# A DLRM tower on one core: features mixed before the projection, row norms from a Gram matrix, products repacked by DMA

## The chip, the core and the metric

The kernel runs on one core of a Trainium2 chip. The core has five engines with an instruction list each: TensorE (PE, matmuls; its weight loads are listed as PEld), VectorE (DVE), ScalarE (ACT), GpSimd (POOL) and SyncE (SP, which here only starts DMAs). They wait for each other by semaphores. The metric is the device time of one execution in microseconds, the median of repeated runs. All arithmetic is float32.

## The reference

512 samples; each has 256 dense features and 26 sparse ids. Each id picks a row of 64 numbers out of a table. Cut to what matters:

```python
e = stack([tbl_f[ids[:, f]] for f in range(26)], axis=1)       # 512 x 26 x 64
x = layer_norm(dense @ Wd.T, gd, bd)                           # 512 x 128
y = layer_norm(einsum('bnd,ed->bne', e, Ws), gs, bs)           # 512 x 26 x 128, norm over e
y = einsum('bne,pn->bep', y, Wsi)                              # 512 x 128 x 32: 26 features mixed to 32
y = swapaxes(layer_norm(y, gsi, bsi), 1, 2)                    # norm over the 32
T = concatenate([x[:, None, :], y], axis=1)                    # 512 x 33 x 128
Z = einsum('bnd,bmd->bnm', T, T)                               # all products of pairs of rows
z = layer_norm(Z[:, TRIL_I, TRIL_J] @ Wl.T, gl, bl)[:, :384]   # 528 pairs -> 512, first 384 kept
h = concatenate([z, dense], axis=1)
h = maximum(h @ W_top1 + b_top1, 0)
h = maximum(h @ W_top2 + b_top2, 0)
out = h @ W_top3                                               # 512 x 1
```

A layer norm subtracts the mean and multiplies by 1/sqrt(variance + 1e-5), then scales (g) and shifts (b).

## The kernel before

The batch is cut into 32 units of 16 samples; 8 units make a block of 128 samples, 4 blocks in all. Every engine's list is written by hand as a loop of steps `step(t)`, in which the stages of different units stand beside each other (unit t in one stage, t-1 and t-2 in later ones). Most buffers are double, by the unit's parity.

A unit goes through these stages. POOL gathers table rows by indirect DMA into `g_sb` (128 rows of 64 numbers each time, two side by side in a slot; 104 gathers). PE turns a slot (`transposes`, L240), ScalarE copies it to `sT` (`rows_out`, L426). PE multiplies by the centred Ws (`project`, L247, two matmuls of 256 columns into `psA`). ScalarE squares and sums each 128 numbers (`squares_a`, L431) and takes the root (L439); VectorE inverts it (L584) and scales by it and by gs into `y1` (`norm_a`, L591). PE mixes the 26 features with the centred Wsi and adds bs by a further row (`mix`, L260, four matmuls of 128 columns into `psB`). ScalarE squares (L446), VectorE sums over 32 (L598), ScalarE takes the root (L452), VectorE inverts it (L603), multiplies into `T` (`norm_b`, L609), and then multiplies `T` by gsi (L615) and adds bsi (L621, or on POOL L221 for every fourth unit). ScalarE puts x into `T` as its first column (`enter_x`, L460). PE forms the products, 16 matmuls of 32x32 (`inner`, L270, into `psZ`), and ScalarE spreads them over the partitions of `Zt` in four copies (`keep_z`, L468):

```python
src = psZ[(m % 2) * PROJ:(m % 2 + 1) * PROJ, :].rearrange("p (s q j) -> p s q j", s=US, j=JQ)
for q in range(4):
    dst = Zt[q * PROJ:(q + 1) * PROJ, u // BU, :, m * US:(m + 1) * US].rearrange("p j s -> p s j")
    last = act.activation(dst, src[:, :, q, :], ACT.Copy)
```

Once a block is there, `linear` (L286) multiplies by Wl in 32 matmuls of 128 columns, cut into pieces that stand in the following steps; `linear_sums` (L294) adds squares, and the three top layers follow (`layer1` L323 and L326, `layer2` L337, `output` L344). The dense part of the first layer (`dense_part`, L305) is computed once. SyncE loads the weights, each behind an early gather; POOL waits for a slot of `g_sb` to be free, as there are 13 slots.

## Time and profile before

| | us |
|---|---|
| time, median of 3 runs | 308.99 (307.81 to 311.92) |
| span of the profiled execution | 212.3 |
| PE busy | 180.5 |
| PE weight loads busy (beside PE) | 155.4 |
| ScalarE busy | 151.7 |
| VectorE busy | 134.3 |
| POOL busy | 110.8 |

The span goes from the first to the last instruction of one profiled execution. That execution's own time is not on record; the timed runs are longer than the span by what lies before and after the program's instructions. Busy times of different engines overlap; the time is set by the chain of waits that ends last.

### The profile page before, as it was taken

To read this page: it belongs to the slowest core of one execution; us is meant where nothing else is said; L and a number is where in the kernel's file an instruction comes from. 1 tells how busy PE (TensorE), PEld (TensorE's weight loads), DVE (VectorE), ACT (ScalarE), POOL (GpSimd) and SP (SyncE) were. 2 spreads that over 40 slices of the span, in tenths; PEclk is the share of its full clock that TensorE was granted. 3 is DMA by queue.
4 is the path that set the end of the run, shared out by engine and by line. 5 is a ranking of instruction groups with operands and counts; after the bars stand their busy time and mean duration, and the time that the engine had idled before them with its cause. 6 is when DMAs were issued, how large, how long until landed. Compare 5 with 4: busy or idle time off the path is not lost.

```text
span 212.3 us, 5428 instructions
## 1 busy us (share of the span) xinstructions
PE 180.5 (85%) x1994; PEld 155.4 (73%) x1994; DVE 134.3 (63%) x360; ACT 151.7 (71%) x597; POOL 110.8 (52%) x116
## 2 busy tenths in 40 slices
PE   0557635879989969998989999899979999999996
PEld 0535433556666658887878998799969999989894
DVE  0234891276878796778877888766777788910401
ACT  2033843889999988999988999967779978590122
POOL 1777777714777677377787867777750200000000
PEclk9985995899999999999999999999999999999999
DMA  5345663310111011101111111111110000000000
GB/s 185 119 124 144 193 210 103 93 47 2 33 26 28 12 27 27 20 19 24 29 23 25 29 25 20 23 30 23 28 25 3 0 3 0 5 3 0 0 3 0
DMA packets 4942, 9.21 MB, mean 43 GB/s; under 512 B 1842, under 2 KB 2098, under 8 KB 4916
## 3 DMA queue, kind: packets, MB, share of 16 engines
q0 software_dynamic: 3328, 3.41, 8.2%
q1 hardware_dynamic: 1298, 4.69, 6.8%
q10 hardware_dynamic: 290, 0.76, 1.0%
q8 instruction: 16, 0.26, 0.6%
q14 instruction: 10, 0.08, 0.1%
HBM read 8.86 MB, written 0.00 MB: 42 GB/s over the span
## 4 chain that ended last, share of the span: by engine, by line
PE 56%; ACT 18%; issue 10%; POOL 9%; DMA 5%; DVE 1%; ACTq 0%
PE psW L286 13%; PE psZ L270 12%; POOL g_sb L214 9%; PE psA L247 8%; ACT Zt L468 7%; PE psB L260 7%; ACT square L431 3%; DMA g_sb<-in_table,row_id 3%; PE psT L240 3%; PE psW L294 2%; DMA ids_sb<-in_ids 2%; PE psA L326 2%; ACT sqB L446 2%; ACT sdB L452 1%; PE psB L326 1%
## 5 line engine op out<-in xcount | busy, mean ns | idle before, releaser
L214 POOL DMA_INDIRECT g_sb<-in_table,row_id x104 | 101.9, 980 | 30.8 <-issue 28.7
L468 ACT ACTIVATE Zt<-psZ 32x128 f32<-32x128 f32 x128 | 48.9, 382 | 4.2 <-PE psZ L270 2.7
L270 PEld LDWEIGHTS psZ<-T 128*32 128x32 f32 x1024 | 34.9, 112 | 10.9 <-issue 8.6
L270 PE MATMUL psZ<-T 128*32 128x32 f32 x1024 | 37.9, 196 | 4.4 <-issue 3.3
L247 PE MATMUL psA<-ws_c,sT 128*104 128x256 f32 x128 | 35.3, 399 | 4.8 <-ACT sT L426 4.4
L431 ACT ACTIVATE square<-psA 104x128 f32<-104x128 f32 x128 | 33.4, 280 | 6.9 <-PE psA L247 6.7
L260 PE MATMUL psB<-wsi_c,y 105*128 105x128 f32 x256 | 36.2, 285 | 0.8 <-DVE y L591 0.4
L591 DVE SCALAR_TENSOR_TENSOR y<-psA,rA,rows_sb 104x128 f32<-104x128 f32 x128 | 35.7, 340 | 0.1
L286 PEld LDWEIGHTS psW<-Zt,wl_sb 128*128 128x128 f32 x256 | 31.4, 192 | 5.9 <-ACT Zt L468 2.8
L286 PE MATMUL psW<-Zt,wl_sb 128*128 128x128 f32 x256 | 32.5, 276 | 3.5 <-ACT hd L554 1.6
L260 PEld LDWEIGHTS psB<-wsi_c,y 105*128 105x128 f32 x256 | 32.4, 197 | 2.9 <-DVE y L591 2.1
L603 DVE RECIPROCAL rB<-sdB 128x16 f32<-128x16 f32 x32 | 8.1, 252 | 39.3 <-ACT sdB L452 39.3
L247 PEld LDWEIGHTS psA<-ws_c,sT 128*104 128x104 f32 x128 | 20.9, 177 | 14.5 <-ACT sT L426 7.6
L426 ACT ACTIVATE sT<-psT 128x256 f32<-128x256 f32 (+1 forms) x32 | 10.8, 338 | 24.0 <-PE psT L240 23.9
L431 ACT ACTIVATION_READ_ACCUMULATOR square<-psA 104x1 f32 x128 | 27.3, 213 | 0.0
L609 DVE TENSOR_TENSOR T<-psB,rB 128x512 f32<-128x512 f32 x32 | 22.0, 687 | 0.5 <-PE psZ L270 0.4
L615 DVE TENSOR_TENSOR T<-T,rows_sb 128x512 f32<-128x512 f32 x32 | 21.8, 681 | 0.1
L598 DVE TENSOR_REDUCE ssB<-sqB 128x16 f32<-128x512 f32 x32 | 21.6, 676 | 0.0
L240 PE MATMUL psT<-small_sb,g_sb 128*128 128x128 f32 x52 | 13.6, 315 | 8.4 <-DMA g_sb<-in_table,row_id 8.4
L221 POOL TENSOR_TENSOR T<-T,rows_sb 128x512 f32<-128x512 f32 x7 | 8.2, 1173 | 23.6 <-DVE T L615 23.6
L446 ACT ACTIVATE sqB<-psB 128x512 f32<-128x512 f32 x32 | 18.8, 586 | 0.6 <-PE psB L260 0.2
L621 DVE TENSOR_TENSOR T<-T,rows_sb 128x512 f32<-128x512 f32 x25 | 17.0, 680 | 0.0
(82 smaller groups left out, 165.0 us busy)
## 6 DMA issues: line engine op xcount, KB each, us to landing
wl_sb<-in_wl SPq DMA_DIRECT2D x4, 512.0 KB, 3.9
g_sb<-in_table,row_id POOLq DMA_INDIRECT x104, 2.5
w_sb<-in_w SPq DMA_DIRECT2D x2, 512.0 KB, 3.5
w_sb<-in_w SPq DMA_DIRECT2D x1, 768.0 KB, 5.9
small_sb<-in_small SPq DMA_DIRECT2D x1, 635.5 KB, 6.2
dense_sb<-in_dense ACTq DMA_DIRECT2D x1, 512.0 KB, 3.8
rows_sb<-in_rows ACTq DMA_DIRECT2D x1, 224.0 KB, 5.4
ids_sb<-in_ids SPq DMA_DIRECT2D x1, 104.0 KB, 4.1
```

The lines of the kernel that those rows point to most:

```text
L214: pool.indirect_dma_start(g_sb[:, k % SLOTS, h * DSP:(h + 1) * DSP], None, table, bass.IndirectOffsetOnAxis(row_id[:, 2 * k + h:2 * k + h ...
L247: mm = pe.matmul(psA[m % 2][0:ROWS, g * 2 * E:(g + 1) * 2 * E], sT[:, (2 * m + g) * ROWS:(2 * m + g + 1) * ROWS], ws_c[:, :], start=True, ...
L260: mm = pe.matmul(psB[m % 2][:, g * P:(g + 1) * P], y1[:, m % 2, g, :], wsi_c[:, :], start=True, stop=True)
L270: mm = pe.matmul(psZ[(m % 2) * PROJ:(m % 2 + 1) * PROJ, s * PROJ:(s + 1) * PROJ], T[:, m % 2, s, 1:1 + PROJ], T[:, m % 2, s, 0:PROJ], star ...
L286: mm = pe.matmul(psW[b % 2][:, f * BS + s0:f * BS + s1], wl_sb[:, j, f * P:(f + 1) * P], Zt[:, b, j, s0:s1], start=(j == 0), stop=(j == JQ ...
L431: last = act.activation(square[0:ROWS, m % 2, g, :], psA[m % 2][0:ROWS, g * E:(g + 1) * E], ACT.Square, accum_out=ssA[0:ROWS, m % 2, g:g + 1])
L446: act.activation(sqB[:, m % 2, :], psB[m % 2][:, :], ACT.Square).then_inc(B_squared, 1)
L468: last = act.activation(dst, src[:, :, q, :], ACT.Copy)
L591: last = dve.scalar_tensor_tensor(out=y1[0:ROWS, m % 2, g, :], in0=psA[m % 2][0:ROWS, g * E:(g + 1) * E], scalar=rA[0:ROWS, m % 2, g:g + 1 ...
L598: dve.tensor_reduce(ssB[:, m % 2, :], sqB[:, m % 2, :].rearrange("p (s j) -> p s j", j=PROJ), AX, ALU.add).then_inc(B_summed, 1)
L609: dve.tensor_tensor(T[:, m % 2, :, 1:], psB[m % 2][:, :].rearrange("p (s j) -> p s j", j=PROJ), rB[:, m % 2, :].rearrange("p (s o) -> p s ...
L615: dve.tensor_tensor(T[:, m % 2, :, 1:], T[:, m % 2, :, 1:], gsi_b.rearrange("p (o j) -> p o j", o=1).broadcast_to([P, US, PROJ]), ALU.mult ...
```

## The change

The stages up to `T` are put in another order, and the unit is now 32 samples (two halves of 16, on partitions 0 to 63 and 64 to 127), 16 units in 4 blocks.

- Mixing comes first: `mix` takes the gathered rows as they lie (`g_sb` as weights, 128 rows) and a masked copy of Wsi for each of the 13 slots of a half block (`wsi_x`) into `psU`, four matmuls of 64 to 192 columns for a unit. Then `project` multiplies by Ws times gs (`ws_g`), and adds bs times the sums of Wsi by matmuls with one row.
- The first norm needs the length of each row after the projection. It is taken from the row itself: `norms` multiplies the turned rows by the 64x64 matrix Ws Ws^T (`gram`), VectorE multiplies by the row and sums over 64 (`mult_a`, `sums_a`), ScalarE takes the root, VectorE inverts it and scales the gathered rows in place (`scale_a`).
- gsi and bsi are no longer applied to `T`. Their products go into the weights of the last linear layer (`wl_g`, and extra rows from `shift_part` and `x_sum`), gl and bl into those of the first top layer (`w1_g`, `bias_part`).
- `inner` forms 32x33 products (a column of ones is in front), in four groups on four ranges of partitions; ScalarE copies each group (8 samples) to `Zs`, and seven DMAs per block (`relay`) put five columns at a time on the partitions of `Zt`. `linear` is then five matmuls of 512 columns with the samples on partitions, its norm is taken by bn_stats on VectorE, and three transposes (`turn`) bring it back.
- All 52 slots of gathered rows are kept; gathers wait for nothing. `psT`, `psG`, `psU`, `psZ`, `psW` and `psH` are single; `psB` is a pair that holds the two halves of one unit. POOL has only the gathers.

```diff
+BLOCKS, BU, HS, US = 4, 4, 64, 16
+UNITS = BLOCKS * BU
+BS = 2 * HS
+SLOTS = HS * NSP // P
+ALL_SLOTS = BLOCKS * SLOTS
+NEW = ((0, 4), (4, 7), (7, 10), (10, 13))
...
+            def relay(b):
+                sp.wait_ge(Z_kept, 4 * BU * (b + 1))
+                if b == 0:
+                    sp.wait_ge(fills, 4)
+                for q in range(7):
+                    sp.dma_start(Zt[BASE[q]:BASE[q] + ROWS[q], b, :, :],
+                                 Zs[FIRST[q] - 1:PROJ, b % 2, CW * q:CW * (q + 1), :]).then_inc(d_zt[b], 16)
...
-            def gathers(lo, hi):
-                for k in range(lo, hi):
-                    if k >= SLOTS:
-                        pool.wait_ge(pair_transposed, k - SLOTS + 1)
-                    for h in range(2):
-                        pool.indirect_dma_start(
-                            g_sb[:, k % SLOTS, h * DSP:(h + 1) * DSP], None, table,
-                            bass.IndirectOffsetOnAxis(row_id[:, 2 * k + h:2 * k + h + 1], 0),
...
+            for k in range(ALL_SLOTS):
+                for h in range(2):
+                    pool.indirect_dma_start(
+                        g_sb[:, k, h * DSP:(h + 1) * DSP], None, table,
+                        bass.IndirectOffsetOnAxis(row_id[:, 2 * k + h:2 * k + h + 1], 0),
+                    ).then_inc(gathered[k], 16)
...
-            def project(u, m):
...
+            def norms(u):
+                lo, hi = NEW[u % BU]
                 pe.wait_ge(sT_ready, u + 1)
-                if u >= 2:
-                    pe.wait_ge(y1_ready, u - 1)
-                for g in range(2):
-                    mm = pe.matmul(psA[m % 2][0:ROWS, g * 2 * E:(g + 1) * 2 * E],
-                                   sT[:, (2 * m + g) * ROWS:(2 * m + g + 1) * ROWS], ws_c[:, :],
+                if u == 0:
+                    pe.wait_ge(gram_ready, 2)
+                else:
+                    pe.wait_ge(A_mul, u)
+                for n in range(hi - lo):
+                    mm = pe.matmul(psG[:, n * P:(n + 1) * P], sT[:, u % 2, n * P:(n + 1) * P], gram[:, :],
                                    start=True, stop=True)
-                mm.then_inc(A_done, 1)
-
-            def mix(u, m):
-                pe.wait_ge(y1_ready, u + 1)
+                mm.then_inc(G_done, 1)
...
-                for g in range(UG):
-                    mm = pe.matmul(psB[m % 2][:, g * P:(g + 1) * P], y1[:, m % 2, g, :], wsi_c[:, :],
-                                   start=True, stop=True)
-                mm.then_inc(B_done, 1)
...
+                ps_ = pieces(j)
+                for n, (c, lo, hi) in enumerate(ps_):
+                    s0 = first_sample(c)
+                    mm = pe.matmul(psU[:, (lo - US * j) * PROJ:(hi - US * j) * PROJ], g_sb[:, SLOTS * b + c, :],
+                                   wsi_x[:, c, lo - s0:hi - s0, :], start=(n == 0), stop=(n == len(ps_) - 1),
+                                   skip_group_check=True)
+                mm.then_inc(U_done, 1)
...
+            def project(u):
+                pe.wait_ge(U_ready, u + 1)
+                if u == 0:
+                    pe.wait_ge(d_bs0, 16)
+                    pe.wait_ge(d_bs1, 16)
+                    pe.wait_ge(x_tr, 1)
+                else:
+                    pe.wait_ge(T_ready, 2 * u)
+                for h in range(2):
+                    pe.matmul(psB[h][:, :], bs_sb[32 * h:32 * h + 1, :], wsum[32 * h:32 * h + 1, :],
+                              start=True, stop=False)
+                for h in range(2):
+                    pe.matmul(psB[h][:, :], ws_g[h * DSP:(h + 1) * DSP, :], U[h * DSP:(h + 1) * DSP, u % 2, :],
+                              start=False, stop=True).then_inc(B_done, 1)
...
-                for s in range(US):
-                    mm = pe.matmul(psZ[(m % 2) * PROJ:(m % 2 + 1) * PROJ, s * PROJ:(s + 1) * PROJ],
-                                   T[:, m % 2, s, 1:1 + PROJ], T[:, m % 2, s, 0:PROJ], start=True, stop=True)
...
+                for gq in range(4):
+                    h = gq // 2
+                    if gq % 2 == 0:
+                        pe.wait_ge(T_ready, 2 * u + h + 1)
+                    if u:
+                        pe.wait_ge(Z_kept, 4 * (u - 1) + gq + 1)
+                    for n in range(GQ):
+                        s = (gq % 2) * GQ + n
+                        mm = pe.matmul(psZ[gq * PROJ:(gq + 1) * PROJ, n * COLS:(n + 1) * COLS],
+                                       T[:, u % 2, h, s, 2:2 + PROJ], T[:, u % 2, h, s, 0:COLS],
+                                       start=True, stop=True)
+                    mm.then_inc(Z_done, 1)
...
-                for n in range(lo, hi):
-                    f, j = n // JQ, n % JQ
-                    mm = pe.matmul(psW[b % 2][:, f * BS + s0:f * BS + s1], wl_sb[:, j, f * P:(f + 1) * P],
-                                   Zt[:, b, j, s0:s1], start=(j == 0), stop=(j == JQ - 1))
...
+                for jj in range(CW):
+                    mm = pe.matmul(psW[:, :], Zt[0:KL, b, jj, :], wl_g[0:KL, jj, :], start=(jj == 0),
+                                   stop=(jj == CW - 1))
...
+            def turn(b):
+                pe.wait_ge(z_normed, b + 1)
+                if b:
+                    pe.wait_ge(y_copied, b)
+                for k in range(KZ):
+                    mm = pe.transpose(psH[:, k * P:(k + 1) * P], zn[:, k * P:(k + 1) * P], eye_sb)
+                mm.then_inc(z_tr, 1)
...
+            def bias_part():
+                pe.wait_ge(d_w1, 16)
+                for f in range(K1):
+                    for k in range(KZ):
+                        mm = pe.matmul(psH[:, f:f + 1], w1_sb[:, k, f * P:(f + 1) * P], bl_c[:, k:k + 1],
+                                       start=(k == 0), stop=(k == KZ - 1))
+                mm.then_inc(bz_done, 1)
+
+            def shift_part():
+                pe.wait_ge(am_ready, 1)
+                pe.wait_ge(d_wl, 16)
+                for jj in range(CW):
+                    mm = pe.matmul(psW[0:NA, :], am[0:KL, jj, :], wl_sb[0:KL, jj, :], start=(jj == 0),
+                                   stop=(jj == CW - 1))
+                mm.then_inc(m_done, 1)
...
+                if t + 1 < UNITS:
+                    transposes(t + 1)
+                if t < UNITS:
+                    mix(t)
+                if t + 1 < UNITS:
+                    norms(t + 1)
+                if 1 <= t:
+                    inner(t - 1)
+                if t < UNITS:
+                    project(t)
+                if t == 0:
+                    x_sum()
+                if t == 1:
+                    shift_part()
                 if t == 2:
...
+                if t in (3, 4):
+                    dense_part(2 * (t - 3))
+                    dense_part(2 * (t - 3) + 1)
+                b, j = (t - 5) // BU, (t - 5) % BU
+                if 0 <= b < BLOCKS - 1:
+                    if j == 0:
+                        linear(b)
+                    if j == 1:
+                        turn(b)
+                        layer1(b, 0, K1 // 2)
+                    if j == 2:
+                        layer1(b, K1 // 2, K1)
+                        layer2(b)
+                    if j == 3:
+                        output(b)
+
+            for t in range(UNITS + 1):
...
+            def rows_out(u):
+                lo, hi = NEW[u % BU]
+                act.wait_ge(tr_done, u + 1)
...
+                act.activation(sT[:, u % 2, 0:(hi - lo) * P], psT[:, 0:(hi - lo) * P], ACT.Copy).then_inc(sT_ready, 1)
...
-            def squares_a(u, m):
-                act.wait_ge(A_done, u + 1)
-                for g in range(UG):
-                    last = act.activation(square[0:ROWS, m % 2, g, :], psA[m % 2][0:ROWS, g * E:(g + 1) * E], ACT.Square,
-                                          accum_out=ssA[0:ROWS, m % 2, g:g + 1])
-                last.then_inc(A_summed, 1)
...
+            def keep_u(u):
...
+                act.activation(U[:, u % 2, :], psU[:, :], ACT.Copy).then_inc(U_ready, 1)
...
-                src = psZ[(m % 2) * PROJ:(m % 2 + 1) * PROJ, :].rearrange("p (s q j) -> p s q j", s=US, j=JQ)
-                for q in range(4):
-                    dst = Zt[q * PROJ:(q + 1) * PROJ, u // BU, :, m * US:(m + 1) * US].rearrange("p j s -> p s j")
-                    last = act.activation(dst, src[:, :, q, :], ACT.Copy)
...
+                lo = 2 * US * j + GQ * gq
+                act.activation(Zs[:, b % 2, 0:COLS, lo:lo + GQ].rearrange("p c s -> p s c"),
+                               psZ[gq * PROJ:(gq + 1) * PROJ, 0:GQ * COLS].rearrange("p (s c) -> p s c", s=GQ),
+                               ACT.Copy).then_inc(Z_kept, 1)
...
+                if t + 1 < UNITS:
+                    rows_out(t + 1)
+                if t < UNITS:
+                    enter_x(t)
+                    keep_u(t)
+                if 1 <= t:
+                    keep_z(t - 1, 0)
+                    keep_z(t - 1, 1)
+                if t + 1 < UNITS:
+                    deviation_a(t + 1)
+                if 1 <= t:
+                    keep_z(t - 1, 2)
+                    keep_z(t - 1, 3)
+                if t < UNITS:
+                    squares_b(t, 0)
+                    squares_b(t, 1)
...
+            def mult_a(u):
+                b, (lo, hi) = u // BU, NEW[u % BU]
+                n = hi - lo
+                dve.wait_ge(G_done, u + 1)
+                dve.tensor_tensor(prod[:, 0:n * P], psG[:, 0:n * P],
+                                  g_sb[:, SLOTS * b + lo:SLOTS * b + hi, :].rearrange("p k d -> p (k d)"),
+                                  ALU.mult).then_inc(A_mul, 1)
+
+            def sums_a(u):
+                n = NEW[u % BU][1] - NEW[u % BU][0]
+                dve.wait_ge(A_mul, u + 1)
+                dve.tensor_reduce(qA[:, 0:2 * n], prod[:, 0:n * P].rearrange("p (m d) -> p m d", d=DSP), AX,
+                                  ALU.add).then_inc(A_sum, 1)
+                dve.wait_ge(A_sum, u + 1)
+                dve.tensor_scalar(qA[:, 0:2 * n], qA[:, 0:2 * n], 0.0, None, ALU.max).then_inc(A_q, 1)
...
+            def scale_a(u):
+                b, (lo, hi) = u // BU, NEW[u % BU]
+                n = hi - lo
+                dve.wait_ge(A_r, u + 1)
+                s = g_sb[:, SLOTS * b + lo:SLOTS * b + hi, :].rearrange("p k (h d) -> p (k h) d", h=2)
+                dve.tensor_tensor(s, s, rA[:, 0:2 * n].rearrange("p (m o) -> p m o", o=1).broadcast_to([P, 2 * n, DSP]),
+                                  ALU.mult).then_inc(s_scaled, 1)
...
-                for g in range(UG):
-                    last = dve.scalar_tensor_tensor(
-                        out=y1[0:ROWS, m % 2, g, :], in0=psA[m % 2][0:ROWS, g * E:(g + 1) * E],
-                        scalar=rA[0:ROWS, m % 2, g:g + 1], in1=gs_b[0:ROWS, :], op0=ALU.mult, op1=ALU.mult)
...
-            def scale_b(u, m):
-                dve.wait_ge(T_normed, u + 1)
-                dve.tensor_tensor(T[:, m % 2, :, 1:], T[:, m % 2, :, 1:],
-                                  gsi_b.rearrange("p (o j) -> p o j", o=1).broadcast_to([P, US, PROJ]),
-                                  ALU.mult).then_inc(T_scaled, 1)
...
+                if 1 <= t <= UNITS:
+                    norm_b(t - 1, 0)
+                    recip_b(t - 1, 1)
+                    norm_b(t - 1, 1)
...
+                    mult_a(t + 1)
+                    sums_a(t + 1)
+                    recip_a(t + 1)
+                    scale_a(t + 1)
...
+                    sums_b(t, 0)
+                    sums_b(t, 1)
+                    recip_b(t, 0)
```

PE's list in the middle of the program, before: one unit of 16 samples in each stage, with an eighth of a block's linear layer (L286). `psB` is the mixed tile, `psA` the projected one.

```order
L260 MATMUL psB<-wsi_c,y 128x128 x4
L247 MATMUL psA<-ws_c,sT 104x256 x2
L286 MATMUL psW<-Zt,wl_sb 128x128 x4
L270 MATMUL psZ<-T 32x32 x16
L240 MATMUL psT<-small_sb,g_sb 128x128
```

And of the change, one unit of 32 samples with the linear layer of a whole block behind it:

```order
L222 MATMUL psT<-small_sb,g_sb 128x128 x3
L248 MATMUL psU<-wsi_x,g_sb 128x128
L248 MATMUL psU<-wsi_x,g_sb 128x192 x2
L248 MATMUL psU<-wsi_x,g_sb 128x96
L233 MATMUL psG<-gram,sT 128x128 x3
L278 MATMUL psZ<-T 32x33 x32
L262 MATMUL psB<-wsum,bs_sb 128x512 x2
L265 MATMUL psB<-U,ws_g 128x512 x2
L292 MATMUL psW<-wl_g,Zt 128x512 x5
```

Projection and products have changed places with mixing, the projection stands last in the step, and `linear` is one piece instead of eight.

VectorE's list in the middle of the program, before, one unit of 16 samples:

```order
L609 TENSOR_TENSOR T<-psB,rB 128x16x32
L591 SCALAR_TENSOR_TENSOR y<-psA,rA,rows_sb 104x128 x4
L615 TENSOR_TENSOR T<-T,rows_sb 128x16x32
L598 TENSOR_REDUCE ssB<-sqB 128x16
L621 TENSOR_TENSOR T<-T,rows_sb 128x16x32
L603 RECIPROCAL rB<-sdB 128x16
L584 RECIPROCAL rA<-sdA 104x4
```

And of the change, one unit of 32 samples:

```order
L632 TENSOR_TENSOR T<-psB,rB 128x16x32
L626 RECIPROCAL rB<-sdB 128x16
L632 TENSOR_TENSOR T<-psB,rB 128x16x32
L594 TENSOR_TENSOR prod<-psG,g_sb 128x384
L601 TENSOR_REDUCE qA<-prod 128x6
L604 TENSOR_SCALAR qA<-qA 128x6
L609 RECIPROCAL rA<-sdA 128x6
L616 TENSOR_TENSOR g_sb<-g_sb,rA 128x384
L621 TENSOR_REDUCE ssB<-sqB 128x16 x2
L626 RECIPROCAL rB<-sdB 128x16
```

The two passes over `T` behind L609 are gone; the sums for the next `T` (L621) now stand behind the whole work for the next unit's row norms.

## Rows read from the trace of the kernel before

**Rows 1.** The page, parts 1 and 2: span, busy time, PE's busy tenths in 40 slices.

```profile
span 212.3 us, 5428 instructions
...
PE 180.5 (85%) x1994; PEld 155.4 (73%) x1994; DVE 134.3 (63%) x360; ACT 151.7 (71%) x597; POOL 110.8 (52%) x116
...
PE   0557635879989969998989999899979999999996
```

**Rows 2.** The page, part 4: the chain that ended last, by engine.

```profile
PE 56%; ACT 18%; issue 10%; POOL 9%; DMA 5%; DVE 1%; ACTq 0%
```

**Rows 3.** Windows: stretch, length, busy PE PEld DVE ACT POOL, clock, DMA, GB/s.

```profile
12.00:34.00 22.00, 11.11 (x54) 8.20 (x54) 14.93 (x47) 10.32 (x50) 16.82 (x18) 0.79 0.60 181
34.00:76.00 42.00, 37.98 (x386) 26.50 (x386) 27.75 (x75) 38.20 (x152) 26.43 (x28) 0.95 0.15 34
76.00:170.00 94.00, 87.82 (x1092) 79.75 (x1093) 72.10 (x191) 82.00 (x336) 61.98 (x62) 1.00 0.12 22
...
189.00:212.30 23.30, 20.94 (x180) 19.66 (x180) 3.21 (x8) 5.34 (x14) 0.00 (x0) 1.00 0.00 1
```

**Rows 4.** The chain in order of time: start, length, records of PE.

```profile
70.40 0.86 PE psW L305 x2
71.26 0.86 PE psA L247 x4
...
73.28 0.38 PE psT L240 x2
...
79.97 0.89 PE psB L260 x8
...
88.92 0.99 PE psB L260 x8
```

**Rows 5.** The timeline from 184 us: 32 products back to back.

```profile
184.67 2.01 PEld L270 LDWEIGHTS psZ<-T 128*32 128x32 f32 x64
```

**Rows 6.** Groups by line and shape: busy, mean ns | idle before.

```profile
L468 ACT ACTIVATE Zt<-psZ 32x128 f32<-32x128 f32 x128 | 48.9, 382 | 4.2 <-PE psZ L270 2.7
...
L591 DVE SCALAR_TENSOR_TENSOR y<-psA,rA,rows_sb 104x128 f32<-104x128 f32 x128 | 35.7, 340 | 0.1
...
L431 ACT ACTIVATE square<-psA 104x128 f32<-104x128 f32 x128 | 33.4, 280 | 6.9 <-PE psA L247 6.7
...
L609 DVE TENSOR_TENSOR T<-psB,rB 128x512 f32<-128x512 f32 x32 | 22.0, 687 | 0.5 <-PE psZ L270 0.4
...
L598 DVE TENSOR_REDUCE ssB<-sqB 128x16 f32<-128x512 f32 x32 | 21.6, 676 | 0.0
...
L446 ACT ACTIVATE sqB<-psB 128x512 f32<-128x512 f32 x32 | 18.8, 586 | 0.6 <-PE psB L260 0.2
...
L452 ACT ACTIVATE sdB<-ssB,eps_c 128x16 f32<-128x16 f32 x32 | 9.8, 307 | 1.9 <-DVE ssB L598 1.2
...
L603 DVE RECIPROCAL rB<-sdB 128x16 f32<-128x16 f32 x32 | 8.1, 252 | 39.3 <-ACT sdB L452 39.3
```

**Rows 7.** The chain at the gathers, and the page's landing time.

```profile
5.55 1.09 POOL g_sb L214
6.94 0.94 POOL g_sb L214
8.19 0.94 POOL g_sb L214
...
27.03 6.89 DMA g_sb<-in_table,row_id
```

**Rows 8.** The page, part 6: issues, KB, us to landing.

```profile
g_sb<-in_table,row_id POOLq DMA_INDIRECT x104, 2.5
```

**Rows 9.** The timeline at the start: VectorE's first use of the weights.

```profile
7.43 0.29 DVE L649 TENSOR_REDUCE means<-small_sb 104x1 f32<-104x128 f32 x1 [6.39 <-DMA small_sb<-in_small]
```

**Rows 10.** The timeline at the end: last output and its DMA.

```profile
209.79 0.60 PE L344 MATMUL psA<-h2T,small_sb 128*1 128x128 f32 x4 [0.19 <-ACT h2T L514]
...
210.74 0.32 SPq L199 DMA_DIRECT2D out_y<-y_sb  x1
```

903 lines of the change are left out of this document (425 added, 478 removed).

## The prediction

> **What bounds the kernel now.** I read the page first [rows 1]. TensorE (PE) is busy for 85% of the span of 212.3 us and reads 9 or 8 in nearly every slice after the first third; ScalarE comes second (71%), VectorE has 63%. The chain that ended last agrees: 56% of it is PE, only 18% ScalarE [rows 2]. The windows show three stages [rows 3]. From 34 to 76 us both PE (38.0 of 42) and ScalarE (38.2 of 42) are full. From 76 to 170 us PE has 87.8 of 94 and sets the pace. After 189 us only PE and a little else works, in series. From 12 to 34 us PE has 11.1 of 22, waiting for weights and gathered rows. The granted clock is 1.00, the 2.4 GHz level, from 76 us on. So a shorter VectorE or ScalarE list pays only where PE is not at its limit, and what counts is PE's own time, the opening and the tail.
>
> The timed median is 308.99 us and the span 212.3 us. The profiled execution has no time of its own on record, so I take 308.99 - 212.3 = 96.7 us as what lies around the span and leave it unchanged. A change within 2% (6.2 us) cannot be told from none here.
>
> **What PE's work costs.** Every f32 matmul is two records. Back to back, 8 records of 128 columns take 0.89 us (0.222 us a matmul), 4 records of 256 columns 0.86 us, 2 records of 512 columns 0.86 us [rows 4]. So a matmul costs 1.68 to 1.74 ns per column, all of them with 104 to 128 contraction rows. Two transposes take 0.38 us. The 32x32 products loaded 64 times in 2.01 us: 32 matmuls, 0.063 us each [rows 5]; with 33 columns I take 2.1 us for 32.
>
> Per 32 samples, before: 3.25 transposes 0.6, four projections of 256 columns 1.7, eight mixings of 128 columns 1.8, products 2.1: 6.2 us. After: transposes 0.6, norms 3.25 x 0.222 = 0.7, four mixing matmuls with 608 columns in all 1.1, products 2.1, and the projection, which is now four matmuls of 512 columns. In series these are 4 x 0.857 = 3.4 us. But they lie on rows 0 to 31 and 32 to 63 (the `bs` rows), then 0 to 63 and 64 to 127 (the two feature halves), in two PSUM banks. No row of the trace has two matmuls on disjoint rows, so their cost is bounded: 3.4 us if nothing coincides (the price of a column in [rows 4]), 1.7 us if each pair coincides wholly. I take the middle, 2.6 us: records start in program order, so of a pair's four records only the second of one half and the first of the other can run side by side, which leaves three record times of four, 2 x 3 x 0.43. The Trainium skill, "TensorE: Matmul & The Clock Gate", Part 3 (What overlaps and what doesn't), says that matmuls on different row groups run at the same time and start strictly in order; no row here shows it. The same skill, "TensorEngine Tiling (Array Packing)", Key Properties, speaks against the change: each change of the tiling mode drains the engine, and this step changes it several times; its price is not in it.
>
> So a unit of 32 costs PE 7.1 us (8.0 in series) against 6.2: +0.9 x 16 = **+15 us**. The last linear layer goes from 32 + 4 matmuls of 128 columns per block (8.0 us) to five of 512 (4.3 us): -3.7 x 4 = **-15 us**. Three transposes per block add 0.57 x 4 = +2.3 us. The weight preparation on PE (`shift_part` five of 512, `x_sum` and `wsum` one each, `bias_part` 12 short ones at 0.22) adds 7 x 0.857 + 2.7 = +8.7 us. In sum PE has **about 11 us more work**, 25 us if the projection is serial.
>
> **What the others give back.** VectorE loses 128 scalings of 340 ns and the two passes over `T` behind L609 (taken at its 687 ns) [rows 6]; per 32 samples it keeps mult, reduce and scale over 416 elements (about 0.6 each), two reduces (0.68), two norms (0.69) and small ones: 5.2 us. ScalarE loses 128 squares (280 ns each, and a read of the sum behind each) and half of the small copies out of `psZ`; it keeps about 5.8 us per 32 (`keep_z`: 264 elements, bounded by 0.38 for 128 and twice that; I take 0.6). Both lie under PE's 7.1 us, so these savings are covered by PE and are worth nothing in the middle, except in the stretch from 34 to 76 us, where ScalarE was full.
>
> **New waits per step.** The step is: transposes(t+1), mix(t), norms(t+1), inner(t-1), project(t). From the first `B_done` of project(t-1) on, ScalarE squares both halves (0.59 each), VectorE reduces (0.68), ScalarE takes two roots (0.31), and VectorE inverts and multiplies (0.25, 0.69 each) [rows 6]. Queued in that order, the first half of `T` is ready 3.3 us later and `rows_out(t+1)`, behind both roots on ScalarE, ends after 3.1 us. Before, the lag of two units and two buffers hid this; now one pair of `psB` banks serves every unit. Norms then end 3.5 us after the projection's end, though PE has only 2.4 us to do. A step without other work is 3.5 + 2.1 + 2.6 = 8.2 us, 1.1 more than PE's work. In the steps of a block:
> - linear: 4.3 us, then bn_stats, root, reciprocal and norm on VectorE stand ahead of norm_b: products begin 7.4 us after the projection, step 12.1;
> - turn and half of layer 1, waiting for `keep_zT` behind the roots: 10.9;
> - half of layer 1, layer 2, with `relu1` and `relu2` between: 11.4;
> - output: 8.3.
> That is **42.7 us per block** of 128 samples (38.5 of it PE's own work). Before, two units of 16 took 88.92 - 79.97 = 8.95 us [rows 4], 36 us for 128 samples, with linear but without layers 1 and 2.
>
> **Gathers.** POOL issues one each 1.25 us (8.19 - 6.94), the first at 5.55 [rows 7]; 104 of them end at 5.55 + 130 = 135.6 us, landing 2.5 us later [rows 8]. No wait holds them now, as there are 52 slots. A unit's share is 6.5 x 1.25 = 8.1 us, less than the mean PE step (10.7), so they bind only in the opening: unit 1 is complete at 5.55 + 14 x 1.25 + 2.5 = 25.5 us, unit 2 at 33, unit 3 at 40.5. Step t begins with the transposes of unit t+1, so project(t) waits for that unit's gathers.
>
> **The sum.** Opening: `small` is there at 7.43 us [rows 9]; behind it VectorE has some 13 us of preparation up to `x_col` (an estimate: two passes over 512 elements at 0.69, four over 128 at 0.34, 25 short ones of up to 192 at about 0.3, and 3 us of waits for PE and ScalarE), so norms(0) ends near 22.5. Project(0) ends at 30, project(1) at 40 (gathers), `shift_part` at 44.6; ScalarE's `m_kept` stands ahead of the roots, so project(2) ends at 52, `bias_part` at 54.6, project(3) 61.8, two dense parts 65.2, project(4) and the rest 75.8, project(5) 83. Two blocks: 83 + 85.4 = 168.4; steps 14 and 15: +12.1 + 10.9 = 191.4. Layer 2 and inner(15): 197.8. Tail, nothing beside it: `keep_z` 0.6, seven relay DMAs (issued at 0.3 to 0.4 us each, as the out DMA's 0.32 [rows 10], landing up to 2.5 later [rows 8]) 4.9, linear 4.4, statistics and norm 2.2, transposes and copy 1.0, layer 1 2.8, relu 0.7, layer 2 1.9, relu 0.6, then 2.5 from the last output's start at 209.79 to the end [rows 1, 10]: 21.6. Span **219.4 us**, 7.1 more than before; time 219.4 + 96.7 = **316.1 us**, +2.3%.
>
> **Rivals.**
> - **Serial projection** (slower): if matmuls on disjoint rows never coincide, each unit pays 0.86 us more, of which 0.35 hides in steps without other work: +12.8 us, 329 us. For it: the matmuls of [rows 4] scale with columns alone. It decides from a projection of 3.0 us on.
> - **The waits are covered better** (faster): if ScalarE's and VectorE's queues run ahead as before, PE's own 38.5 us per block holds: -4.2 x 2.5, and the opening a few less: span about 205 to 209, 302 to 306 us. If the pairs also coincide wholly, another -0.86 x 11 = -9: 295 us, where the gathers (last landing 138 us, plus tail and one and a half blocks' side work) begin to bind. It decides where span falls under 206. For it: VectorE (5.2 us) and ScalarE (5.8) have room beside PE's 7.1. Against it: single `psB`, and the strict order above.
> - **Opening starves** (slower): before, one gather landed after 6.9 us [rows 7] while weights were loading. `wl` is now one load of 1.3 MB between units 1 and 2. Up to +6 us twice: about 325 us.
>
> **Chances.** Forecast 0.43, its own range 311 to 321, about half of it within 2% (0.20) and half above (0.23). Serial 0.28, slower. Better covered 0.19, nearly all faster (0.16). Starved opening 0.10, slower. So faster 0.16, same 0.23, slower 0.61. The range takes in the serial case with 3 us more and the better covered one down to PE's own work, and leaves out whole coincidence: 302 to 332 us.
>
> **What will show it.** Group L262/L265: the pitch from one project's start to its end, 2.6 or 3.4 us. VectorE near 85 us busy, ScalarE near 95, PE near 180 or more. Waits: PE on `T` (L632) or on `sT` (L440) before norms and products; the last relay 5 us; the last gather near 136 us, not on the chain. I am wrong altogether if the part around the span moves, or if steps without side work are under 7.1 us.

## The result

The changed kernel takes **338.74 us** (median of 4 runs, 336.73 to 340.87), the kernel before 309.19 us (4 runs, 307.81 to 311.92): ratio 1.096, 95% interval 1.089 to 1.102, slower. 316.1 us were forecast, in a range that ended at 332.

One thing is needed to read this. The profile shown ahead of the prediction (span 212.3 us) is of an execution unlike the timed ones. A profiled execution of the same kernel among timed runs has a span of 309.6 us at 311.45 us, so only 1.8 us lie around the span. Runs were made in sets, each on one chip. In the result's own set (its chip is not on record) and in the first three sets of experiments (chips 3, 8 and 3) the kernel before took 308 to 313 us; in the fourth and fifth, on chips 6 and 5, it took 211 and 210 us. I call the first kind of chip "holding" and the second "free". That is a name and not a finding: the free sets were also the last ones, so chip and time can't be told apart. Some executions of a set take about 2% longer at a lower granted clock; the medians keep these and the ratios leave them out.

The page of the changed kernel on a holding chip, parts 1 and 2, to be read against [rows 1]:

```profile
span 337.9 us, 4417 instructions
...
PE 193.7 (57%) x1749; PEld 129.2 (38%) x1749; DVE 106.6 (32%) x256; ACT 101.7 (30%) x224; POOL 101.5 (30%) x109
...
PE   0648503000000000019999999889998899986276
...
POOL 3777777777777777200000000000000000000000
```

TensorE (PE) reads 0 for ten slices of 8.4 us, some 85 us, and they end about where GpSimd's (POOL's) gathers end. Two windows of it, columns as in [rows 3]:

```profile
60.00:90.00 30.00, 2.35 (x11) 1.39 (x11) 0.00 (x0) 0.60 (x1) 22.68 (x25) 0.50 0.14 26
...
152.00:338.00 186.00, 161.26 (x1612) 108.08 (x1611) 81.30 (x181) 91.84 (x203) 0.00 (x0) 0.93 0.04 8
```

PE gets through 11 matmul records in 30 us, and the clock falls to 0.50, the 1.2 GHz level, after PE has hardly worked. The trace shows nobody that it waits for ("issue"). The timeline of PE has products (`inner(0)`), each record 0.21 us long, starting 2.80 us apart:

```profile
111.28 0.21 PE L278 MATMUL psZ<-T 128*32 128x33 f32 x1 [2.59 <-issue]
114.08 0.21 PE L278 MATMUL psZ<-T 128*32 128x33 f32 x1 [2.59 <-issue]
116.88 0.21 PE L278 MATMUL psZ<-T 128*32 128x33 f32 x1 [2.59 <-issue]
```

And whoever waits for PE waits long. In ScalarE's timeline `keep_u(1)` (L453) starts at 73.49 us, though mix(1) stands in PE's rows as done at 38.3:

```profile
73.49 0.60 ACT L453 ACTIVATE U<-psU 128x512 f32<-128x512 f32 x1 [21.05 <-remote]
135.09 0.60 ACT L487 ACTIVATE Zs<-psZ 32x264 f32<-32x264 f32 x1 [61.00 <-remote]
```

"Remote" means that the trace names no releaser on this core. Signals from ScalarE to VectorE arrive at once (squares end at 39.77 us, the sum over them starts at 39.80). I call this the **hold-up**. From 152 us on PE works as usual, and from there to the end it takes 186 us.

The kernel before, profiled on a holding chip, has the same in pieces. POOL's gathers pause wherever it waits for a slot, and PE's high readings lie in the pauses:

```profile
span 309.6 us, 5428 instructions
...
PE   0650507884259724984299348964599499999997
...
POOL 3777740027700672057702760177205600100000
```

### The profile page after: what moved, and what is told of

The parts are those of the page before. It is cut to its first block, busy times and chain, and to the rows that moved or that the text cites. A ratio compares the mean times of both kernels' runs of the same rounds, so it can differ in the third digit from the quotient of the medians.

```text
span 337.9 us, 4417 instructions
## 1 busy us (share of the span) xinstructions
PE 193.7 (57%) x1749; PEld 129.2 (38%) x1749; DVE 106.6 (32%) x256; ACT 101.7 (30%) x224; POOL 101.5 (30%) x109
## 4 chain that ended last, share of the span: by engine, by line
PE 49%; issue 33%; ACT 4%; DVE 4%; POOL 4%; DMA 3%; SPq 1%; ACTq 0%
PE psZ L278 11%; PE psW L292 6%; PE psB L265 6%; PE psB L262 6%; POOL g_sb L209 4%; PE psU L248 4%; PE psG L233 4%; DVE ssB L621 3%; PE psH L325 2%; PE psW L313 2%; PE psW L359 2%; ACT sqB L459 1%; PE psT L222 1%; PE psH L351 1%; DMA ids_sb<-in_ids 1%
## 5 line engine op out<-in xcount | busy, mean ns | idle before, releaser
L278 PE MATMUL psZ<-T 128*32 128x33 f32 x1024 | 38.9, 198 | 89.4 <-issue 89.4
L487 ACT ACTIVATE Zs<-psZ 32x264 f32<-32x264 f32 x64 | 39.5, 618 | 91.3 <-remote 77.3
L621 DVE TENSOR_REDUCE ssB<-sqB 128x16 f32<-128x512 f32 x32 | 20.6, 682 | 37.8 <-ACT sqB L459 31.3
L233 PE MATMUL psG<-gram,sT 128*128 128x128 f32 x104 | 17.8, 317 | 16.2 <-issue 14.1
L292 PE MATMUL psW<-wl_g,Zt 127*128 127x512 f32 x40 | 20.6, 666 | 8.2 <-DMA Zt<-Zs 8.2
L609 DVE RECIPROCAL rA<-sdA 128x6 f32<-128x6 f32 (+1 forms) x16 | 3.1, 194 | 68.2 <-ACT sdA L447 67.8
L459 ACT ACTIVATE sqB<-psB 128x512 f32<-128x512 f32 x32 | 17.5, 596 | 18.9 <-PE psB L265 12.0
L248 PE MATMUL psU<-wsi_x,g_sb 128*128 128x192 f32 (+4 forms) x128 | 22.5, 323 | 0.0
L233 PEld LDWEIGHTS psG<-gram,sT 128*128 128x128 f32 x104 | 15.3, 221 | 17.6 <-issue 14.2
L248 PEld LDWEIGHTS psU<-wsi_x,g_sb 128*128 128x128 f32 x128 | 21.2, 209 | 0.0
L265 PE MATMUL psB<-U,ws_g 64*128 64x512 f32 x64 | 20.0, 703 | 0.0
L262 PE MATMUL psB<-wsum,bs_sb 1*128 1x512 f32 x64 | 19.9, 701 | 0.0
L453 ACT ACTIVATE U<-psU 128x512 f32<-128x512 f32 x16 | 9.5, 594 | 28.4 <-remote 21.0
L313 PE MATMUL psW<-zT,w_g 128*128 128x128 f32 x96 | 12.5, 281 | 4.1 <-ACT zT L501 4.1
```

The costliest lines, as they stand in the source:

```text
L233: mm = pe.matmul(psG[:, n * P:(n + 1) * P], sT[:, u % 2, n * P:(n + 1) * P], gram[:, :], start=True, stop=True)
L248: mm = pe.matmul(psU[:, (lo - US * j) * PROJ:(hi - US * j) * PROJ], g_sb[:, SLOTS * b + c, :], wsi_x[:, c, lo - s0:hi - s0, :], start=(n = ...
L262: pe.matmul(psB[h][:, :], bs_sb[32 * h:32 * h + 1, :], wsum[32 * h:32 * h + 1, :], start=True, stop=False)
L265: pe.matmul(psB[h][:, :], ws_g[h * DSP:(h + 1) * DSP, :], U[h * DSP:(h + 1) * DSP, u % 2, :], start=False, stop=True).then_inc(B_done, 1)
L278: mm = pe.matmul(psZ[gq * PROJ:(gq + 1) * PROJ, n * COLS:(n + 1) * COLS], T[:, u % 2, h, s, 2:2 + PROJ], T[:, u % 2, h, s, 0:COLS], start= ...
L292: mm = pe.matmul(psW[:, :], Zt[0:KL, b, jj, :], wl_g[0:KL, jj, :], start=(jj == 0), stop=(jj == CW - 1))
```

## The experiments

All ratios are to the kernel before on the same chip, with 95% intervals.

### First set, a holding chip: pauses between the gathers

**before_again**, the kernel before unaltered.

> The kernel before, unchanged, to see its span beside its time. Theory A (a fixed part of 96.7 us lies around the span, as the prediction took it): span near 212 us again, time 309. Theory B (almost nothing lies around the span, as in the changed kernel with 337.9 of 339.7 us; the engines crawl while gathers are queued, and the one profile of before happened to miss it): span near 307 us, with a stretch of some 95 us in which PE is nearly idle.

Measured: 308.66 us, span 309.6 in the profiled run of 311.45. Theory B holds, but the idle time of PE lies in pieces and not in one stretch. The idea that 96.7 us lie around the span fell here.

**a_lead3**, the changed kernel with

```
+                if u >= LEAD:
+                    pool.wait_ge(tr_done, u - LEAD + 1)
```

ahead of the gathers of unit u (LEAD is 3).

> The changed kernel, but POOL holds a unit's gathers until the transposes of three units before it are done. Theory B1 (gathers issued without a pause starve the other engines' semaphores and issue; between 54 and 150 us one record each 0.7 to 1.4 us): the crawl is gone or much shorter, time 220 to 260 us. Rival B2 (the crawl comes from something else in the list, such as instruction fetch at that place): unchanged within 2%, 338 us.

Measured: 330.8 us, ratio 1.073 (1.064 to 1.082). Neither forecast: it is 2.3% less. The hold-up broke into pieces as in the kernel before, but lost only 8 us of its length.

**b_free**, the kernel before with 52 slots for gathered rows, no waits on POOL, and POOL's shifts done by VectorE (`on_pool` false, `gathers(0, PAIRS)`).

> The kernel before with 52 slots for gathered rows, no wait of POOL for a free slot, and no shifts on POOL (VectorE does all 32, some 5 us more for it). Theory B1: the crawl gets as long as in the changed kernel, time 20 us or more over 309. Rival B2: same as before, 305 to 315 us.

Measured: 326.7 us, ratio 1.057 (1.049 to 1.064). The mirror image in kind, though not the full 20 us of theory B1: it stands 17.5 us above the result's 309.2, 18.4 above the kernel before in its own set, and by its expectation some 5 of these can be the shifts. Without pauses the kernel before is held up in one block, to 151 us, and then needs 173 us.

**a_inflight2**, the changed kernel, POOL waiting for the landing of the slot before last.

> The changed kernel, but POOL waits, before the two gathers of a slot, until those of the slot two before have landed. If the number of gathers in flight is the cause: 220 to 260 us. If it is POOL's steady stream of issues (one each 1.25 us) whatever is in flight: 330 us or more, as landings take 2.5 us and the wait hardly slows the stream.

Measured: 331.9 us, ratio 1.074 (1.067 to 1.082). This was forecast for the case that the number in flight has no part in it. The test is weak: the wait hardly changed the stream, which runs at one gather per 1.25 us from 43 us on and ends at 139.9 us (137.1 unaltered).

### Second set, a holding chip: the gathers taken away

**a_pooldma**: each gather a plain DMA of the same 128 rows of 256 bytes.

```
-                    pool.indirect_dma_start(g_sb[...], None, table, IndirectOffsetOnAxis(...))
+                    pool.dma_start(g_sb[...], table[(2 * k + h) * P:(2 * k + h + 1) * P, :])
```

> The changed kernel; GpSimd's 104 indirect gathers are replaced by 104 plain DMAs of the same size, from the same engine's queue: 128 consecutive rows of the table instead of the rows that the ids name, so the looked-up rows are left out. Theory: TensorE's crawl (one record per 0.70 us from 38 to 150 us in the changed kernel) comes with the indirect gathers alone; then this run has no crawl and takes 218 to 226 us (186 us of work after the crawl's end in the changed kernel plus some 38 us before it). Rival 1: it comes with GpSimd feeding a DMA queue, of whatever kind; then the crawl lasts as long as GpSimd issues, 300 us or more if it still needs 1.25 us for one. Rival 2: it comes with the DMAs' traffic of 128 short rows; then about 330 us here and with SyncE as the issuer.

**a_spdma**: the same DMAs issued by SyncE.

> The changed kernel with the gathers replaced by 104 plain DMAs of the same size (128 consecutive rows of the table; the looked-up rows are left out), issued by SyncE, GpSimd idle after its one addition. Theory (the crawl belongs to GpSimd's gathers): 218 to 226 us, and TensorE's idle time 'issue' of 89.4 us before psZ gone. Rival (the traffic of short rows does it): still 300 us or more.

**b_spdma**: the kernel before, treated as a_spdma.

> The kernel before with its 104 gathers replaced in the same way (128 consecutive rows for each, the looked-up rows left out, SyncE issues them, GpSimd keeps its shifts). Theory: without the crawl it takes 208 to 216 us, near the 212.3 us span of the profile of before that had none, and stands 6 to 14 us below the changed kernel without gathers; so the change's own work costs 3 to 6%, and of the measured gap of 29.6 us the larger part, 15 to 24 us, is how much of the crawl each kernel pays. Rival (the change's own work is what costs): the two kernels without gathers still stand 25 to 35 us apart.

Measured: 222.8, 222.0 and 203.3 us; the kernel before, gathering, took 313.0 beside them (ratios 0.712, 0.706, 0.651). The hold-up is gone in all three, as forecast, and both rivals of a_pooldma with it: neither POOL as the issuer nor rows of 256 bytes do it by themselves. What went is the indirect gather: the looking up of rows by id and POOL's work of issuing it; no run parts these two. Of b_spdma both forecasts failed: it was to take 208 to 216 us and stand 6 to 14 (or 25 to 35) below a_spdma; it took 203.3 and stands **18.7** below. Pages of a_spdma and b_spdma:

```profile
span 220.1 us, 4418 instructions
...
PE 178.5 (81%) x1749; PEld 120.6 (55%) x1749; DVE 106.4 (48%) x256; ACT 101.3 (46%) x224; POOL 0.6 (0%) x5
```

```profile
span 201.1 us, 5447 instructions
...
PE 175.5 (87%) x1994; PEld 152.4 (76%) x1994; DVE 133.7 (67%) x360; ACT 151.5 (75%) x597; POOL 8.8 (4%) x12
```

PE's busy time differs by 3 us, its idle time by 16 (41.6 against 25.6): mostly waits, not work. Part of it lies in the opening. The waits of PE in the profile that was read first (span 212.3 us), and in a_spdma:

```profile
PE psT L240 <- DMA g_sb<-in_table,row_id: 8.4, 4, 5.4
```

```profile
PE psB L364 <- DVE xn L712: 5.8, 1, 5.8
...
PE psU L246 <- DVE g_sb L614: 2.4, 1, 2.4
```

The kernel before waits 8.4 us for gathered rows in that profile, where nothing is held up, and b_spdma has none of this wait. The changed kernel waits for its gathers too, but with plain DMAs it waits 8.2 us for VectorE's preparation instead, and gains nothing.

**a_defer**, another order alone: `T` held for six units, no products until step 3, two units' products in steps 4 to 6.

> The changed kernel with another order alone: T held for six units instead of two, no products (inner) in the steps 0 to 3, two per step from 4 to 6, then one as before; bias_part one step later, dense_part one step later. Nothing is left out. Theory (while GpSimd gathers, TensorE completes one record per 0.70 us whatever its size): the 128 records of inner(0) that filled the crawl give way to the projection, the mix and the norms of two to three units, about 50 records each; their 23 us of work at full pace are then done by 150 us, less some 5 us of new wait ahead of linear(0): 312 to 322 us. Rival (TensorE stands still while GpSimd gathers, or the crawl is the products' own, however many there are): in the first case 336 to 345 us, in the second under 290 us.

Measured: 341.1 us, ratio 1.089 (1.083 to 1.095), as good as no change (338.7 is 1.096). My law, a record per 0.70 us, was wrong in its unit. In this trace ScalarE and VectorE see PE's results at 85.1 (mix, 8 matmul records), 101.9 (norms, 6), 118.7 and 124.3 (projection, 6 and 2) and 148.8 us (`shift_part`, 10): 2.5 to 2.8 us per matmul record whatever its size, where the small products have 2.80. So only some 36 records pass in 100 us. What passed here instead of `inner(0)` is worth 8.7 us at full pace (mix 1.1, norms 0.9, projection 2.1, `shift_part` 4.6); less 1.9 for the products and 5.5 that `linear(0)` now waits longer, 1.3 us are left. By the ratios, from different chips, it gained 2. The forecast of 312 to 322 us failed, and the time fits the rival's first case; but PE didn't stand still.

### Third set, a holding chip: fewer gathers, and gathers strung out

**a_half**: POOL gathers the even slots, SyncE fills the odd ones with plain DMAs.

> The changed kernel with half of the indirect gathers: the even slots are gathered by GpSimd as before (52 gathers), the odd slots are filled by SyncE with plain DMAs of 128 consecutive table rows (their looked-up rows are left out). With 104 gathers it took 338.7 us, with none 222.0 us. Theory (the time lost is proportional to the gathers, 1.12 us for each): 277 to 284 us. Rival (a fixed price, or one that sets in only once the gathers have gone on for some 25 us, since the changed kernel's crawl first shows at 30 to 38 us): about 255 us if 25 us of each run of gathers are free, over 300 us if the price is fixed.

Measured: 267.9 us (2 runs), between the two forecasts: 0.88 us per gather instead of 1.12. The price goes by the number of gathers, though not strictly: it fits that the first of a long row cost less.

**a_spread**, nothing left out; each slot's two gathers wait for a point in PE's unit four earlier:

```
+                n = k % SLOTS - NEW[u % BU][0]
+                s = u - 4
...
+                if n == 0:
+                    pool.wait_ge(tr_done, s + 2)
+                if n == 1:
+                    pool.wait_ge(G_done, s + 2)
+                if n == 2 and s > 0:
+                    pool.wait_ge(Z_done, 4 * s - 1)
+                if n == 3:
+                    pool.wait_ge(B_done, 2 * s + 2)
```

> The changed kernel with the gathers of each slot tied to a step of TensorE four units earlier (the transposes, the norms, the products, the projection of that unit), so that GpSimd gathers two at a time, 2.5 us, and then waits; nothing is left out. Theory 1 (every microsecond in which GpSimd gathers costs TensorE nearly all of it, in pieces of whatever length): 325 to 338 us, as with the pauses of one unit's length (330.8 us). Theory 2 (the crawl sets in 2 to 3 us after a run of gathers begins, as the 5 us bins of the trace of the kernel before suggest, 30 matmuls in the first bin of a run against 1 to 3 later): pieces of 2.5 us hardly slow TensorE, 240 to 280 us.

**b_spread**, the kernel before with its gathers given out by the unit.

> The kernel before with its gathers given out unit by unit (one or two slots, 2.5 to 5 us, each time the transposes of the unit five earlier are done) instead of six or seven slots every fourth unit; GpSimd's shifts stay where they were; nothing is left out. Theory 1: 300 to 315 us, no change. Theory 2 (short runs of gathers do little harm): 220 to 260 us.

Measured: a_spread 292.9 us, ratio **0.938** (0.932 to 0.944), between its two forecasts and the one complete kernel that beats both on a holding chip; b_spread 312.7 us, ratio 1.003 (1.000 to 1.006). Their pages:

```profile
span 291.0 us, 4417 instructions
...
PE   0825710489798969697979697979799999882665
...
POOL 2787776443415353606161555161520000000000
```

```profile
span 312.2 us, 5452 instructions
...
PE   0650507885239923991369636975399579999997
...
POOL 3777740027710573037700771067502700100000
```

In a_spread the first 34 gathers still come in a row, up to 50 us; from then on they come in twos and fours with waits between. PE then reads 6 to 9 while POOL reads 0 to 6: short runs of gathers cost PE less than a long one. In b_spread POOL's 7s still stand in rows: the gathers queued up behind a shift on POOL that was waiting for VectorE, and came out together. It is no test of short runs.

**a_sp_nobs**: a_spdma without the bias's two matmuls per unit (`bs` is missing from the sum).

> The changed kernel without gathers (plain DMAs from SyncE, 222.0 us) and without the bias's part of the projection: the two 512-column matmuls of bs and wsum per unit are left out, so bs is missing from the sum. They take 16 times 1.06 us in the steady state and 2.0 us in the first two units, 19.0 us in the trace without gathers. Theory (TensorE's list sets the time of every step, so these records count in full): 203 to 206 us. Rival (the steps are as long as the round trip from the projection through ScalarE and VectorE back to T, and the bias's matmuls fill waits): 214 to 222 us.

Measured: 212.1 us by the median. The profiled spans compare better, as their clocks are alike (0.934, and 0.938 in a_spdma, on another chip, neither held up): 207.8 against 220.1 us, 12.3 less. So it lies between both forecasts: of these 19 us of records about 12 counted in full, and about 7 filled waits.

### Fourth and fifth sets, free chips

**a_spread3**, **a_single** and **a_single_2** tie the gathers of the changed kernel to PE's points at three units' distance, in pairs or singly; **b_fine** and **b_fine_2** do so for the kernel before, in pairs, with each shift of unit u moved behind the gathers of step u + 1. **after_again** is the changed kernel unaltered.

> The changed kernel with its gathers in pairs as in the run at 292.9 us, each pair tied to a step of TensorE three units earlier instead of four, and those of the third unit tied to the first norms, mix and projection; so the first run of gathers is some 16 instead of 26. Nothing is left out. Theory (a gather costs TensorE 1.1 us when the gathers follow one another without a gap for long, about half of that in pairs with a gap; of the 71 us that the run at 292.9 us still stands above the kernel without gathers, some 27 belong to the first 22 gathers in a row): 283 to 290 us. Rival (the longer distance of four units was what helped, as cover for the late signals): 295 us or more.

> As the run before this one, but every single gather has a wait of its own for one of seven points in TensorE's unit (transposes, mix, norms, two of the products, both halves of the projection). Nothing is left out. Theory (the shorter a run of gathers, the less each of them costs): 265 to 283 us. Rival (a gather's cost is fixed once there is any gap): within 3 us of the run with pairs.

> The kernel before with each slot's two gathers tied to a step of TensorE five units earlier (products for the first slot of a unit, the mix for the second), and each of GpSimd's shifts placed so that no gather queues up behind it; in the run with gathers given out by the unit they still came in runs of 12, 15 us long, because they had queued up behind a shift. Nothing is left out. Theory (short runs of gathers cost half): 203 us without gathers plus 104 gathers at 0.5 to 0.7 us, 255 to 276 us. Rival (this kernel's steps of 5.6 us leave hardly a gap between 3.25 gathers of 1.25 us, 4.1 us in all, so the runs join up again): 300 us or more.

> The changed kernel once more, unaltered, next to the kernel before on the same chip. The kernel before has run at 308 to 313 us in some calls and at 211 us in another; both kinds are forecast. Where the kernel before takes some 310 us (TensorE is held up by gathers): 336 to 343 us, ratio 1.08 to 1.10. Where it takes some 211 us (it is not): 219 to 225 us, ratio 1.04 to 1.07; the rival there is that only the kernels with strung-out gathers escape, and this one still takes over 300 us.

> The changed kernel with every single gather tied to a point of TensorE's unit, once more. Where the kernel before takes some 310 us: 265 to 283 us if short runs of gathers cost less each, 288 us or more if it is any gap that counts. Where it takes some 211 us: 220 to 225 us, as the last time.

> The kernel before with each slot's two gathers tied to a step five units earlier and no gather behind a shift, once more. Where the kernel before takes some 310 us: 255 to 276 us if short runs of gathers cost half, 300 us or more if the runs join up. Where it takes some 211 us: 210 to 213 us, as the last time.

Measured, fourth set: before **211.3** us; a_spread3 223.3 us, ratio 1.059 (1.051 to 1.067); a_single 221.9, 1.053 (1.043 to 1.063); b_fine 211.4, 1.004 (1.000 to 1.009). Fifth set: before **209.9**; after_again **221.9** us, ratio **1.057** (1.048 to 1.066); a_single_2 224.5; b_fine_2 212.4, 1.014 (1.007 to 1.021). Nothing is held up here, so these runs could not tell how much single gathers save; that stays open, and so does whether the kernel before would gain from it. They hardly tried it, either: with PE at full pace the points are passed early, and the gathers come in runs of 34, 12 and 14 in b_fine and of 40, 6 and 14 in a_spread3. The forecasts of the fourth set had a holding chip in mind and failed; in the fifth, the three for a free chip were met. What the runs settle is the change without the hold-up: +12 us, 5.7%, and after_again's rival, that the unaltered change is held up everywhere, is out. No variant beats the kernel before on a free chip.

## Why the prediction was wrong, point by point

**The step that failed** is "I take 308.99 - 212.3 = 96.7 us as what lies around the span and leave it unchanged". Around the span lie 1.8 us. Nearly all the rest of the 96.7 was the hold-up, which the profile I read did not have. The hold-up is not constant either: by medians the kernel before pays 309.2 - 209.9 = 99 us for it, the changed one 338.7 - 221.9 = 117. Of the 29.5 us between the kernels, 12 are then the change's own cost and 17.5 more hold-up. This split isn't firm. It compares different chips, and measured against the kernels without gathers (222.0 and 203.3 us, one chip) the change's own cost is 18.7 and only some 11 us are more hold-up. Either way the hold-up grew, and the 96.7 didn't stay as it was. The prediction's own sign of being "wrong altogether", that the part around the span moves, came true.

**Why it pays more.** "No wait holds them now", I wrote of the gathers, and counted that as free. On a holding chip it is what costs. With the pauses taken out (b_free, which also moves the shifts) the kernel before pays 17 us more; with pauses put in (a_lead3) the changed one pays 8 less, with short runs (a_spread) 46 less.

**The span without the hold-up** was forecast at 219.4 us; after_again has 219.0 (220.8 us in all). That closeness is luck: up to the end of inner(15) it is 6.7 us faster than forecast, and the tail is 6.3 us slower. And the base of 212.3 us was read at a granted clock of 0.968; at 1.00 the kernel before has spans of 207.0 to 208.1 us on the free chips. So the change without the hold-up cost 11 to 12 us and not the 7.1 of the sum. Windows of after_again against [rows 3], and its steps:

```profile
34.00:76.00 42.00, 41.70 (x412) 27.32 (x411) 26.23 (x59) 25.46 (x56) 31.95 (x34) 0.96 0.20 44
76.00:170.00 94.00, 86.07 (x947) 60.07 (x946) 49.55 (x110) 53.77 (x123) 47.88 (x51) 1.00 0.14 28
...
198.00:219.00 21.00, 13.74 (x59) 8.21 (x59) 2.00 (x5) 2.01 (x5) 0.00 (x0) 0.83 0.01 2
...
199.69:204.50 4.81, 4.81 (x6) 2.18 (x7) 0.00 (x0) 0.00 (x0) 0.00 (x0) 0.50 0.01 3
```

```profile
120.55 1.13 PE L262 MATMUL psB<-wsum,bs_sb 1*128 1x512 f32 x4
121.60 1.13 PE L265 MATMUL psB<-U,ws_g 64*128 64x512 f32 x4
122.66 4.56 PE L292 MATMUL psW<-wl_g,Zt 127*128 127x512 f32 x10
...
163.48 4.56 PE L292 MATMUL psW<-wl_g,Zt 127*128 127x512 f32 x10
```

- *Projection, 2.6 us a unit:* it takes 122.66 - 120.55 = 2.11 us. Two pairs of 512-column matmuls on disjoint rows take 1.06 us each, where a pair in series took 2 x 0.86 [rows 4]. So they coincide more than "three record times of four"; the rival with the serial projection is out. By this term alone, +15 us for the units becomes +7. The Trainium skill, "TensorE: Matmul & The Clock Gate", Part 3, says that matmuls on different row groups run at once; the 1.06 us agree. The Trainium skill also says, in "TensorEngine Tiling (Array Packing)", Key Properties, that a change of the tiling mode drains the engine; whatever such changes within the projection cost is inside the 2.11.
- *A block, 42.7 us:* 163.48 - 122.66 = 40.8 us; its four steps take 11.4, 10.8, 11.0 and 7.6 (forecast 12.1, 10.9, 11.4, 8.3). PE is busy for 37.0 of it and idle for 3.8, where the forecast had 38.5 and 4.2. So the new waits are there nearly as forecast, and the cheaper projection makes the difference; over the whole run PE waits 4.1 us for `zT`, 4.5 for `h1T`, 2.4 for `sT`.
- *Opening:* project(0) ends at 32.8 (30 forecast), project(5) at 81.8 (83). PE waits four times for gathered rows, 8.5 us in all, which binds only here, as forecast. The longest of these waits (5.5 us, up to 20.3) is what the rival of the starved opening spoke of; the kernel before has the same (5.4), and the opening as a whole came out 2.8 us late.
- *inner(15)* ends at 191.1 instead of 197.8, after the cheaper blocks.
- *Tail, 21.6 us:* it takes 27.9. This is the term that was too small:

```profile
189.23 1.83 PE L278 MATMUL psZ<-T 128*32 128x33 f32 x61
...
192.50 5.09 SPq L193 DMA_DIRECT2D Zt<-Zs  x7
...
199.69 7.00 PE L292 MATMUL psW<-wl_g,Zt 127*128 127x512 f32 x10 [8.22 <-DMA Zt<-Zs]
208.94 0.55 PE L301 MATMUL psH<-small_sb,zn 128*128 128x128 f32 x3 [2.25 <-DVE zn L650]
```

The last copies and the relay hold PE for 8.2 us instead of 5.5: issuing the seven DMAs takes 5.09 us, 0.73 each, where I had taken 0.3 to 0.4 from the output's DMA. After this idle stretch the granted clock is 0.50, the 1.2 GHz level, for 4.8 us, and the linear layer takes 7.00 us against 4.56 in the middle of the kernel.

- *VectorE near 85, ScalarE near 95 us busy:* 107.0 and 101.5. PE's waits in the steady part name ScalarE and not VectorE, so this cost nothing there; which of VectorE's groups I had sized too small is not worked out.
- *Last gather near 136 us:* issued at 137.1.

**Where the 12 us come from.** In its last 23.3 us the kernel before has PE busy for 20.9 [rows 3], since the layers of two blocks are left over as filling. The changed kernel has kept none: in its last 27.9 us PE waits for 11.9 (8.2, 2.25, 0.69 and 0.72). PE's whole busy time is 177.5 us, 3 below the 180.5 of [rows 1]:

```profile
span 219.0 us, 4417 instructions
...
PE 177.5 (81%) x1749; PEld 121.2 (55%) x1749; DVE 107.0 (49%) x256; ACT 101.5 (46%) x224; POOL 102.7 (47%) x109
...
PE   0562499999999999979798997979899979705774
```

Without gathers it is 3 above (178.5 and 175.5). So the forecast "about 11 us more work" was too much by 8 or more, and the sign of what is left can't be told. By this reading the change trades ScalarE's and VectorE's load, which had little effect on the time, for a chain at the end with a DMA in it. It rests on the two traces; no run moved work into the tail to prove it.

## What to carry to other kernels

A large gap between a profiled span and the timed median is a finding, not a constant: profile the kernel again among timed runs before anything is added to it. If one engine's starts are evenly spaced with "issue" ahead of them, and its waiters say "remote", look for what another engine does in just that stretch, and take that away as the first experiment. And waits that look useless on a side engine may be what spaces its work out; removing them is a change to be priced.

## What the hardware showed that I had not expected

- In the sets that I call holding, while GpSimd issues indirect gathers back to back (one per 1.25 us), TensorE completes one matmul record per 2.5 to 2.8 us whatever its size, and its signals reach other engines up to 35 us after the ends that the trace gives its records. 104 gathers cost 99 to 117 us. On a free chip the gathers cost the changed kernel nothing (221.9 us with them; 222.0 without, on a holding chip) and the kernel before some 7 us (209.9 and 211.3 against 203.3), which by the traces is mainly its wait for rows in the opening; these pairs are on different chips. 104 plain DMAs of as many rows, from GpSimd's queue or SyncE's, cause no hold-up on a holding chip.
- The pace of the gathers themselves doesn't change. But in held-up stretches the trace has 5 to 10 increments of semaphores by DMAs per 5 us, where a free chip's has 64 for the same four gathers. The others must have arrived, since the transposes wait for all of them; it is their records that are missing. PE's starts there lie 2.10, 2.80 or 3.50 us apart, in steps of 0.70. A path that signals or their records share is therefore what I would suspect; no run isolated it. One rival is open: every execution here, timed or profiled, has a recorded span, so no run shows the kernels without recording, and the recording itself may have a part in the hold-up. Whether it is the chip or its state at the time stays open too.
- The hold-up depends on spacing: 1.12 us per gather in one row of 104; 1.05 with 34 in a row and then runs of 6 to 8; 0.68 with 34 in a row and then twos and fours.
